# P transposed ahead of keys and values, x1 held with the convolution's rows outermost

## The reference

```python
y  = einsum('boi,bih->boh', agg_w, x) + agg_b[:, :, None]    # agg_w, agg_b: 8 weight sets mixed by softmax(MLP(cond))
q, k, v = y @ Wq, y @ Wk, y @ Wv                             # 32 query heads, 8 key/value heads of 16
x1 = x + softmax(causal(rope(q) rope(k)^T / 4)) v @ Wo       # attention inside a sequence of 32 rows
z  = conv1d(x1, weight, pad 4, 9 taps, 4 groups) + cond @ c_weight^T + bias   # over the 512 columns
out = x1 + z @ base_W^T + base_b + 2 * lora(z)               # 8 low-rank experts of rank 16, weighed by a router on z
```

## Time and profile before

| what | value |
|---|---|
| median of three runs | 609.29 us (609.05 to 610.1) |
| the profiled execution | 612.12 us |
| its span, from the first to the last instruction | 610.3 us |
| TensorE busy, matmuls | 586.5 us |
| TensorE busy, weight loads | 493.8 us |
| VectorE busy | 494.5 us |
| ScalarE busy | 221.4 us |
| GpSimd busy | 225.9 us |
| DMA traffic | 71.26 MB in 122086 packets |

### The profile page before, as it was taken

How to read it: one execution, slowest core, us unless ns; L and a number is a source line. 1 busy time by engine, 2 the same in 40 slices (tenths; PEclk the granted TensorE clock), 3 DMA queues, 4 the chain that set the end, 5 groups by cost and what they waited for, 6 DMA issues and landing times.

```text
span 610.3 us, 14252 instructions
## 1 busy us (share of the span) xinstructions
PE 586.5 (96%) x4937; PEld 493.8 (81%) x4937; DVE 494.5 (81%) x1236; ACT 221.4 (36%) x603; POOL 225.9 (37%) x182
## 2 busy tenths in 40 slices
PE   5789999999999999999999999999999999999986
PEld 4577888888889888888888888888888888898864
DVE  4658788888888888888888888888888888888855
ACT  4344333333333333334333433333333334334321
POOL 7344244333333433233344333343443333334310
PEclk9879999999999999999999999999999999999999
DMA  8547553445555434455553345455534455554241
GB/s 186 109 145 158 117 130 107 94 113 112 116 133 133 116 96 111 99 112 133 133 133 109 90 111 111 113 133 133 129 101 97 107 117 117 133 133 112 64 112 59
DMA packets 122086, 71.26 MB, mean 117 GB/s; under 512 B 45661, under 2 KB 104189, under 8 KB 121944
## 3 DMA queue, kind: packets, MB, share of 16 engines
q1 hardware_dynamic: 120576, 70.53, 48.7%
q0 software_dynamic: 144, 0.28, 0.3%
q10 hardware_dynamic: 1352, 0.27, 0.2%
HBM read 51.53 MB, written 19.53 MB: 116 GB/s over the span
## 4 chain that ended last, share of the span: by engine, by line
PE 78%; DMA 10%; DVE 5%; SPq 3%; issue 2%; ACT 1%; ACTq 1%; DVEq 0%
PE ps L435 17%; PE ps L602 15%; PE ps L623 9%; DMA scratch<-x_dram 6%; PE ps L629 5%; PE ps L665 5%; PE ps L539 4%; PE ps L657 4%; PE ps L684 3%; PE ps L706 3%; PE ps L576 3%; PE ps L673 2%; PE ps L613 2%; PE ps L579 2%; DVE x1p L1290 1%
## 5 line engine op out<-in xcount | busy, mean ns | idle before, releaser
L1013 POOL TENSOR_TENSOR qk<-network,t 128x640 f32<-128x640 f32 x31 | 48.3, 1558 | 162.6 <-DVE t L1206 162.6
L435 PE MATMUL ps<-wqkv_hi,y_hi 128*128 128x512 f32 (+1 forms) x256 | 87.8, 343 | 0.9 <-POOL y_lo L1003 0.5
L435 PE MATMUL ps<-wqkv_lo,y_hi 128*128 128x512 f32 (+1 forms) x256 | 87.4, 342 | 0.0
L435 PE MATMUL ps<-wqkv_hi,y_lo 128*128 128x512 f32 (+1 forms) x256 | 87.4, 342 | 0.0
L1025 POOL TENSOR_TENSOR raw<-x1p,basebB 128x512 f32<-128x512 f32 x32 | 49.5, 1547 | 57.8 <-DVE x1p L1290 57.6
L799 ACT ACTIVATE raw<-ps 128x512 f32<-128x512 f32 x64 | 37.7, 595 | 76.0 <-PE ps L684 75.9
L1020 POOL TENSOR_TENSOR raw<-raw,zero 128x512 f32<-128x512 f32 x32 | 33.3, 1040 | 73.9 <-DVE raw L1279 73.9
L435 PEld LDWEIGHTS ps<-wqkv_hi,y_hi 128*128 128x128 f32 x256 | 48.8, 191 | 8.8 <-ACT y_hi L799 2.0
L997 POOL TENSOR_TENSOR raw<-raw,rz 128x512 f32<-128x512 f32 x32 | 33.6, 1049 | 59.4 <-DVE rz L1235 59.4
L435 PEld LDWEIGHTS ps<-wqkv_lo,y_hi 128*128 128x128 f32 x256 | 48.9, 191 | 6.1
L435 PEld LDWEIGHTS ps<-wqkv_hi,y_lo 128*128 128x128 f32 x256 | 48.8, 191 | 6.0
(11 more groups left out here) (204 smaller groups left out, 1468.9 us busy)
## 6 DMA issues: line engine op xcount, KB each, us to landing
scratch<-x_dram SPq DMA_DIRECT2D x96, 256.0 KB, 5.8
x_dram<-x1p SPq DMA_DIRECT2D x32, 260.0 KB, 2.0
xm<-x SPq DMA_DIRECT2D x32, 256.0 KB, 4.4
xr<-x SPq DMA_DIRECT2D x32, 256.0 KB, 2.7
out<-raw SPq DMA_DIRECT2D x32, 256.0 KB, 2.1
v_dram<-vS SPq DMA_DIRECT2D x32, 64.0 KB
vB<-v_dram SPq DMA_DIRECT2D x128, 16.0 KB, 4.8
mixb<-mixb_dram SPq DMA_DIRECT2D x28, 64.0 KB, 3.9
```

Of the source, the lines that this page charges most:

```text
L435: last = mm(dst, a, b, start=(n == 0), stop=(n == 3 * len(left) - 1))
L1013: nc.gpsimd.tensor_tensor(qk[:, :], t1, t2[:, :], ALU.add).then_inc(qk_sb, 1)
```

## The change

Five things are changed.

1. In steps 3 to 30 TensorE transposes P before it computes keys and values of t + 1. ScalarE makes both copies of transposed P before it copies the routing weights.
2. The transposed routing weights lie in bank 3 except for the last three groups, and `values` no longer waits for their low half.
3. The waits of `values` for vB and for prT become a function, `values_ready`. It is called before `conv`, except in step 1 (after it) and step 31 (directly before `values`).
4. The two-column matmul is gone.
5. `x1_dram` has the row as its outermost dimension. SP writes it in four DMAs, one for each phase j, with runs of 130 values (520 bytes), and reads it in three DMAs with one run of 16 x 130 - 2 = 2078 values (8312 bytes) in each of 32 partitions. `xc` has a pitch of 130 instead of 128 values. The counts of `x1_out` grow fourfold.

```diff
-        xc = scratch[0:SHIFTS * S, 0:NB * PH * P].rearrange("p (q n) -> p q n", n=P)
+        xcs = scratch[0:SHIFTS * S, 0:NB * PH * (P + 2)]
+        xc = xcs.rearrange("p (q n) -> p q n", n=P + 2)[:, :, 0:P]
...
-        x1_dram = nc.dram_tensor("x1_dram", [NB * PH, CG * PH, P + 2], F32, kind="Internal").ap()
+        x1_dram = nc.dram_tensor("x1_dram", [CG * PH, NB * PH, P + 2], F32, kind="Internal").ap()
...
+        def hwT_bank(u):
+
+            return 7 if isinstance(u, int) and u >= G - 3 else 3
+
+        def keys_late(t):
+
+            return not isinstance(t, int) or 3 <= t < G - 1
...
                 if live(t - 1):
-                    sp.wait_ge(x1_out, 16 * t)
+                    sp.wait_ge(x1_out, 16 * PH * t)
+                    run = NB * PH * (P + 2) - 2
                     for s in range(SHIFTS):
-                        sp.dma_start(xc[S * s:S * (s + 1), :, :],
-                                     x1_dram[:, :, s:s + P].rearrange("q r n -> r q n")).then_inc(xc_in, 16)
+                        sp.dma_start(xcs[S * s:S * (s + 1), 0:run],
+                                     x1_dram.rearrange("r q n -> r (q n)")[:, s:s + run]).then_inc(xc_in, 16)
...
                 if live(t):
                     sp.wait_ge(x1_sb, t + 1)
-                    sp.dma_start(x1_dram.rearrange("q (i j) n -> (q i) j n", j=PH), x1p[:, :, :]).then_inc(x1_out, 16)
+                    for j in range(PH):
+                        sp.dma_start(x1_dram.rearrange("(i j) q n -> j q i n", j=PH)[j], x1p[:, j, :]).then_inc(x1_out, 16)
...
+            def values_ready(t):
+
+                pe.wait_ge(vB_in, 16 * HK * (t + 1))
+                pe.wait_ge(pT_sb, 2 * t + 2)
+
             def values(t):
 
-                pe.wait_ge(vB_in, 16 * HK * (t + 1))
-                if live(t - 2) and not peeled(t, G - 1):
-                    pe.wait_ge(hwT_lo_sb, t - 1)
                 if peeled(t, 0):
                     pe.wait_ge(prep_sb, 1)
                 if peeled(t, 1):
                     pe.wait_ge(base_lo_sb, 3)
-                pe.wait_ge(pT_sb, 2 * t + 2)
-                if not isinstance(t, int):
-                    mm(ps[0:S, 4, 0:2], convW[:, 0, :, :].rearrange("p j o -> p (j o)"), xc[:, 0, 0:2], start=True, stop=True)
...
-                nc.tensor.transpose(ps[:, 7, 0:P], hw[:, :, :].rearrange("p e r -> p (e r)"), ident).then_inc(hwT_ps, 1)
+                nc.tensor.transpose(ps[:, hwT_bank(u), 0:P], hw[:, :, :].rearrange("p e r -> p (e r)"), ident).then_inc(hwT_ps, 1)
...
                 if live(t + 1):
                     queries(t + 1)
+                if live(t + 1) and not keys_late(t):
                     keys_values(t + 1)
...
                 if live(t):
                     transpose_p(t)
+                if live(t + 1) and keys_late(t):
+                    keys_values(t + 1)
                 if peeled(t, G - 1):
+                    values_ready(t)
                     values(t)
...
+                if live(t) and not peeled(t, G - 1):
+                    if not peeled(t, 1):
+                        values_ready(t)
                 if live(t - 1) and not peeled(t, G):
                     conv(t - 1)
+                if peeled(t, 1):
+                    values_ready(t)
                 if live(t) and not peeled(t, G - 1):
                     values(t)
...
                 if live(t):
                     transposed_p(t, 0)
-                if live(t) and peeled(t, G - 1):
+                if live(t):
                     transposed_p(t, 1)
                 if live(t - 2) and not peeled(t, G - 1):
                     high_hwT(t)
-                if live(t) and not peeled(t, G - 1):
-                    transposed_p(t, 1)
...
-                    wait(dve, x1_out, 16 * (t - 1))
+                    wait(dve, x1_out, 16 * PH * (t - 1))
```

4 lines of the change are left out of this document (2 added, 2 removed).

## The result

The changed kernel takes **780.09 us** (median of four runs, 773.51 to 788.2) against 609.32 for the kernel before on the same chip: a ratio of 1.276, 95% interval 1.268 to 1.285. The forecast was 628 us, its range 601 to 645. The sign was right and the size was off by an order of magnitude: +171 us where +19 was forecast. The profiled execution took 788.2 us (span 786.4).

What follows compares the result with a forecast made beforehand. TensorE, busy 96%, was taken as the bound. Stall 0.43 + 1.14 - 0.65 = 0.92 us, net of 0.28 saved +0.64, times 26 = +16.6; with the other iterations +18.7 us, giving 628 us on the median's scale, range 601 to 645.

Steps and rivals of the forecast that it cites:

- narrow matmul and hidden wait: TensorE: dropping the two-column matmul (0.15) and the waits behind the convolution (0.13) saves 0.28 us in each of 27 iterations.
- wait for vB ahead of the convolution: TensorE: the fourth vB load lands on average 0.43 us after the convolution's start, so the moved wait costs 0.43 us.
- four writes, shift of the queue: SP's queue: three more writes at 0.38 us each push the loads and reads behind them back by 1.14 us.
- long runs in the reads: x1 reads: 96 runs of 8.3 KB for 1536 of 512 B gain 0.65 us, the middle of 0 and 1.3.
- The swap of P with keys and values, and bank 3: TensorE: P asked for 1.41 us earlier, no wait for ScalarE's copy; routing weights in bank 3; both priced at 0.
- The lower bound of the text: TensorE: only the dummy matmul's 27 x 0.15 = 4.1 us is saved if the convolution needs 1.01 us.
- the text's upper bound of 1.5: SP's queue: shift of 1.5 us from four writes if each brings a pause of its own on the engines.
- The bound of 381 GB/s: x1 reads: at the rate read for the base weights' 8 KB runs, 768 KB would take 2.0 us, 1.3 less.
- the first rival: DMA chain: faster x1 reads bring vB in before the convolution; 604.2 us, or 601.5 on the median's scale; chance 0.35.
- the third: DMA chain: a stall of 0.28 us eats just what the dummy gave; 609 to 610 us; chance 0.07.
- The second: x1 reads: destination width sets the rate, long runs give nothing, stall 1.57 us; 648 us; chance 0.15.
- The signs listed: Trace checks: values 0.88 us after the convolution's start, stalls of 0.9, period near 18.2, reads issued 1.1 us later.

Runs made afterwards that it cites:

- order alone: Kernel before with only the new TensorE order (P first, value waits ahead of the convolution, hwT in bank 3, no narrow matmul), x1 written and read as before: 623.5 us.
- changed with short runs: Changed kernel, but its three x1 reads fetch runs of 128 elements (512 bytes) again, same layout and places: 780.6 us.
- the three loads out of the way: Changed kernel with xr, the bias and xm issued behind the x1 reads and the vB loads: 644.9 us; the same with short-run reads: 718.0 us.
- four writes alone: Kernel before, old layout and short-run reads, but x1 written by four DMAs, one for each j, instead of one: 650.2 us.
- candidate: Kernel before with P ahead of keys and values, value waits ahead of the convolution's last matmul, no narrow matmul, xm behind reads and vB loads: 605.7 us.

## Why the prediction failed, step by step

The sum was a stall of 0.92 us a step, net +0.64. Measured: 5.70. Three terms failed: the granted clock, which the sum left at nothing without a reason and which cost 2.33 us a step; the four writes, put at 1.14 and measured at 2.24; and the reads, put at a gain of 0.65 where they lost 0.62. Term by term, from the table:

| term | forecast | measured | from |
|---|---|---|---|
| narrow matmul and hidden wait | -0.28 | -0.13 | C, order alone against before |
| wait for vB ahead of the convolution | +0.43 | +0.62 | R, order alone against before |
| four writes, shift of the queue | +1.14 | +2.24 | W, changed against before |
| long runs in the reads | -0.65 | +0.20 | R, changed against changed with short runs |
| new layout and the loads ahead of the reads | 0 | +0.42 | R, changed with short runs against order alone |
| granted clock | 0 | +2.33 | C, changed (7.54) against order alone (5.21) |
| sum | +0.64 | +5.68 | step: 5.70 |

- **The swap of P with keys and values, and bank 3, at 0: right.** P is transposed at 313.54 without a wait, and the wait for ScalarE's copy is gone.
- **Narrow matmul: the size was off.** The lower bound of the text (the convolution needs 1.01 us before any other shape of tile) is what happened: 1.00. Rows 5 were read as the convolution's length; they end at the narrow matmul, which follows sooner than the values do.
- **Wait for vB: the right mechanism, nearly the right size.** The 0.43 was where vB landed; the convolution begins 0.22 us behind a landing (mean of the order run's steps 4 to 28).
- **Four writes: mis-sized by two.** The term took 0.38 us an issue from two static DMAs. A quarter into the old layout costs 0.44, into the new 0.62, so the shift is 2.24, beyond the text's upper bound of 1.5. That bound was drawn from pauses of the engines, and the trace had no row for a write in three dimensions. The 2.0 us landing of x1 hid nothing, since SyncE itself was late; and with the three loads out of the way the landing of the four writes alone keeps W at 4.06.
- **Long runs in the reads: forecast as a gain, worth nothing here.** In the changed kernel they change R by +0.20 and the time not at all, in the old layout R by +0.24; only with the three loads out of the way do they win, 1.07 us. The bound of 381 GB/s was a misread row. In that half microsecond the trace has no 8 KB packet (the view of DMA from 37.5 to 38 us):

```profile
DMA packets 109, 0.19 MB, mean 381 GB/s; under 512 B 16, under 2 KB 16, under 8 KB 109
```

  They are the 2 KB rows of xr and xm, issued at 35.47 and 36.11. The base weights, 1 MB issued at 36.58, landed 8.2 us later, some 128 GB/s with other loads beside them. So no row of before held the rate of 8 KB runs, and the middle between 0 and 1.3 us had no upper end; the first rival stood on the same row.
- **The reads' other part, which no term held: +0.42.** It holds the new layout and what is in flight ahead of the reads. In step 31, where only the end of the vB loads is beside them, the reads of before were issued from 578.0 to 579.2 and landed at most 4.5 us later, 5.7 in all; in the changed kernel:

```profile
L404 SPq DMA_DIRECT2D scratch<-x_dram x3: 421/434/594, 747.1 to 748.2; - x3
...
DMA to landing us min/median/max: 3.7/4.3/4.9
```

  That is 1.1 + 4.9 = 6.0 us, 0.3 more, where the forecast wanted 0.65 less. The rule of the Trainium skill that the prediction set beside its sum ("SBUF — State Buffer", section "Door 1: The DMA port swizzle": 32 partitions reach half of the ports) fits the missing gain. No run shows that it is the cause: the prediction took the ranges 0 to 31 and 0 to 63 from it while the third read goes into 64 to 95, no run varies the partitions, and with a clear queue the run length did change the landing (7.1 against 5.9 us).
- **The clock: missing.** The text had PEclk at 1.00 and never asked what a stall does to it. With the forecast stall of 0.9 us a step it would have stayed near that, by the nearest runs (order alone, 0.5 us idle: 0.997; four writes alone, 0.9 us lost a step: 0.985). Behind over 3 us it stands at half, and 57 us of the 171 are its by the medians. With it the step's net loss is nine times the forecast; without it, 3.37 us, five times.
- **The rivals.** The first (DMA chain short enough) and the third (balance) are out. The second (width sets the rate and long runs give nothing, 648 us) was nearest on the reads, whether or not the width is the cause, and still missed by 132 us for the clock and the queue's shift. None of the rivals had the queue's shift above 1.5 us.
- **The signs listed.** Reads on the clock of rows 8 were to be issued 1.1 us later: 2.2. A stall of 0.9 and a period of 18.2: 3.2 and 23.3. Values 0.88 behind the convolution: 1.83 at the lowered clock, 1.00 at full.

## What to carry to other kernels

When a loop already runs at the bound of one engine with a chain of transfers 0.5 us behind it, every issue put ahead of the critical read is paid in full once that slack is gone (four writes in the old layout: 1.43 us of shift, 0.94 us of loss). Cost an issue by its own shape, not by the nearest one, and issue what is not urgent (bias, xm, xr) behind what the next matmul waits for. Ask of each forecast stall whether it is long enough to lower TensorE's clock, since a stall of 3 us cost another 2.3 us of slow matmuls. A wait that moves up in an engine's order stands in front of everything behind it: ahead of the convolution it cost 0.6 us of R. Ahead of the last of four matmuls that run side by side it was hardly cheaper where it bound (0.12 us), and free only where the load had landed before (in the candidate 0.8 us ahead of the convolution). And look at the packets of a stretch before its rate is taken as the rate of one load.

## What the runs showed of the hardware

- SyncE's issue time follows the pattern's shape, not the bytes: 0.32 to 0.36 us for the old write of 260 KB, 0.44 for a quarter of it in the old layout, 0.62 for the same quarter in the new one, 0.59 for the whole in one write of four dimensions.
- The same 260 KB land in 2.0 us in the old layout and in 4.6 in the new one when written at once.
- A broadcast of 64 KB issued 1.4 us ahead of the reads delays them by 1.2 us, a load of 256 KB to 128 partitions 0.5 us ahead (xm) by 0.9, one 2.0 us ahead (xr) by nothing; kind and place aren't separated.
- In the matmuls of 96 rows by 32 columns that make the convolution, the fourth held back by 0.75 us pushes what follows back by nearly as much: the four overlap.
- Three reads of 512-byte runs take 7.1 us from the new layout and 5.6 from the old one, at the same size and target partitions; open why.
- Twelve matmuls a step that only fill the idle stretch raise the mean granted clock from 0.881 to 0.981 and save 57 us of 780.
